# A loop hint on every engine: the closing branch of each loop is announced at the head of its body

## The reference

```
x = _layernorm(x + _L0_attn_ref(x, L0_attn_W), axis=-1)
x = _layernorm(x + _L0_ffn_ref(x, ...), axis=-1)
x = _layernorm(x + _L1_attn_ref(x, ...), axis=-1)
x = _layernorm(x + _L1_ffn_ref(x, ...), axis=-1)
```

```
h = dA_t * h + dBx_t
y = jnp.einsum('bdn,bn->bd', h, C_t)
```

## Time and profile before

| | |
|---|---|
| median of 3 runs | 2109.95 us |
| the three runs | 2109.95, 2128.29, 2106.08 us |
| the profiled execution, its own time | 2105.13 us |
| span, first to last instruction | 2103.4 us |
| mean granted TensorE clock | 0.852 |
| PE busy | 1455.2 us (69%) |
| DVE busy | 1404.4 us (67%) |
| POOL busy | 1285.9 us (61%) |
| ACT busy | 947.2 us (45%) |

### The profile page before, as it was taken

One profiled execution on the slowest core, in us unless ns is written; L12 is line 12 of the kernel. 1 busy time (PEld: TensorE's weight loads), 2 busy tenths in 40 slices (PEclk: granted clock), 3 DMA queues, 4 the chain that ended last, 5 costly groups with the idle time before them and its releaser, 6 DMA issues.

```text
span 2103.4 us, 22098 instructions
## 1 busy us (share of the span) xinstructions
PE 1455.2 (69%) x5345; PEld 863.5 (41%) x5345; DVE 1404.4 (67%) x2613; ACT 947.2 (45%) x1612; POOL 1285.9 (61%) x927
## 2 busy tenths in 40 slices
PE   4777400443898878888787898888766639968772
PEld 3655300331343333333333343333444418857661
DVE  3666597111799989989898898999844413335554
ACT  2443100112655665655565664565433317746461
POOL 2111201672998989988899998888645660053664
PEclk8999655556899999999999999999977759988996
DMA  5333481232322233222233222242023115857673
GB/s 151 110 107 109 129 217 27 39 41 55 123 89 101 108 117 116 80 88 75 107 116 116 85 82 77 105 147 106 5 83 109 48 46 160 228 159 212 191 222 85
DMA packets 215268, 229.96 MB, mean 109 GB/s; under 512 B 24456, under 2 KB 182216, under 8 KB 210760
## 3 DMA queue, kind: packets, MB, share of 16 engines
q1 hardware_dynamic: 192392, 203.28, 30.3%
q0 software_dynamic: 22784, 25.71, 6.0%
HBM read 168.37 MB, written 62.95 MB: 110 GB/s over the span
## 4 chain that ended last, share of the span: by engine, by line
PE 29%; issue 21%; DVE 19%; POOL 10%; another core or an unknown queue 8%; ACT 6%; DMA 3%; SPq 2%; DVEq 1%; POOLq 0%; ACTq 0%
DVE hst L1557 9%; PE bank L1208 8%; POOL dbx L752 5%; PE bank L1163 4%; DMA wv<-packed_weights 2%; PE bank L1073 2%; PE bank L1313 1%; PE bank L1299 1%; PE bank L1296 1%; POOL xe L686 1%; PE bank L1322 1%; PE bank L1161 1%; PE bank L1197 1%; DVE prod L1573 1%
## 5 line engine op out<-in xcount | busy, mean ns | idle before, releaser
L1557 DVE TENSOR_TENSOR_SCAN hst<-bank,dbx 128x512 f32<-128x512 f32 x512 | 592.3, 1206 | 55.6 <-ACT bank L949 40.9
L752 POOL TENSOR_TENSOR dbx<-u,ball 128x1024 f32<-128x1024 f32 x256 | 615.2, 2474 | 4.7 <-POOL u L783 2.8
L1208 PE MATMUL bank<-prod,ident 128*128 128x512 f32 x1024 | 502.9, 626 | 21.0 <-DVE prod L1573 17.8
L949 ACT ACTIVATE bank<-dt,aneg 128x511 f32<-128x511 f32 x512 | 347.5, 689 | 314.9 <-DVE hst L1557 314.7
L1208 PEld LDWEIGHTS bank<-prod,ident 128*128 128x128 f32 x1024 | 203.1, 201 | 252.0 <-issue 200.6
L1573 DVE TENSOR_TENSOR prod<-hst,bank 128x1024 f32<-128x1024 f32 x192 | 233.6, 1217 | 18.7 <-DVE hst L1557 13.4
L814 POOL DMA_INDIRECT yg<-expert_rows,row_of x128 | 125.0, 976 | 166.1 <-DMA expert_rows<-yu 116.1
L761 POOL TENSOR_TENSOR prod<-hst,call 128x1024 f32<-128x1024 f32 x64 | 158.9, 2482 | 70.4 <-DVE hst L1557 70.3
L1192 PE MATMUL bank<-parts,sel_c 128*128 128x512 bf16 x192 | 75.1, 392 | 113.5 <-DVE prod L1573 112.8
L1597 DVE SCALAR_TENSOR_TENSOR hg<-bank,wv,ha 128x256 f32<-128x256 f32 x96 | 42.1, 480 | 157.1 <-remote 56.7
L647 POOL TENSOR_SCALAR rstd<-mv 128x4 f32<-128x4 f32 x16 | 3.7, 228 | 199.9 <-DVE mv L1377 199.9
(11 more groups left out here) (262 smaller groups left out, 2915.8 us busy)
## 6 DMA issues: line engine op xcount, KB each, us to landing
ball<-b_rows SPq DMA_DIRECT2D x32, 2048.0 KB, 7.1
wv<-packed_weights SPq DMA_DIRECT2D x96, 322.0 KB
call<-b_rows SPq DMA_DIRECT2D x16, 1024.0 KB, 9.5
xr<-sorted_rows SPq DMA_DIRECT2D x48, 256.0 KB
expert_rows<-yu SPq DMA_DIRECT2D x48, 256.0 KB
xg_rows<-xg SPq DMA_DIRECT2D x16, 320.0 KB, 2.6
xt<-in_x SPq DMA_DIRECT2D x16, 256.0 KB, 3.0
xT<-in_xT SPq DMA_DIRECT2D x16, 256.0 KB, 3.2
```

What stands on the lines that cost most here:

```text
L752: gp.tensor_tensor(dbx[n % NDB][:, :, :], u[s.par][:, :, :], ball[:, n:n + 1, :].to_broadcast([P, NH, SEQ]), ALU.mult).then_inc(dbx_rdy, 1)
L949: act.activation(da_ps[h][:, 1:SEQ], dt_[s.par][:, h, 1:SEQ], ACT.Exp, scale=aneg[:, h, n:n + 1]).then_inc(da_rdy, 1)
L1208: last = mm(y_ps[:, h, :], ident[:, :], from_[:, h, :], start=False, stop=(n == NS - 1), skip_group_check=True)
L1557: dve.tensor_tensor_scan(h_of[:, h, :], da_ps[h][:, :], dbx[n % NDB][:, h, :], 0.0, ALU.mult, ALU.add).then_inc(scan_rdy, 1)
```

## The change

Every loop is built with the same loop function, called with a flag that it had left off. With the flag, the first instruction of the body is a branch hint: it names the branch that closes the loop, and with it the place that it jumps to. Nothing else is moved. All fourteen loops get one hint instruction in the body, which is carried out in every turn.

```diff
@@ schedule (Mamba, called by all five engines)
-    with eng.Fori(0, NB // 2 - 2) as j:
+    with eng.bass.Fori(0, NB // 2 - 2, engines=(eng.engine,), hint_back_edge=True) as j:
         for i in (2, 3):
             iteration(Seq(j, i + 1), Seq(j, i), Seq(j, i - 1), Seq(j, i + 2))
@@ stage 1: the same edit for sp, gp, act, pe and dve
-            with dve.Fori(0, NB // 2 - 1) as j:
+            with dve.bass.Fori(0, NB // 2 - 1, engines=(dve.engine,), hint_back_edge=True) as j:
@@ expert groups: the same edit for gp, act, pe and dve
-            with gp.Fori(0, E0 // EG // 2 - 1) as j:
+            with gp.bass.Fori(0, E0 // EG // 2 - 1, engines=(gp.engine,), hint_back_edge=True) as j:
```

More of the change, by code:

```diff
@@ L461, in _ @@
             load_x(Seq(0, 1))
-            with sp.Fori(0, NB // 2 - 1) as j:
+            with sp.bass.Fori(0, NB // 2 - 1, engines=(sp.engine,), hint_back_edge=True) as j:
                 for i in (1, 2):
@@ L651, in _ @@
             rsqrt(rstd, mv, Seq(0, 0), mv_rdy, rstd_rdy)
-            with gp.Fori(0, NB // 2 - 1) as j:
+            with gp.bass.Fori(0, NB // 2 - 1, engines=(gp.engine,), hint_back_edge=True) as j:
                 for i in (1, 2):
@@ L871, in _ @@
             stage1(Seq(0, 0), None)
-            with act.Fori(0, NB // 2 - 1) as j:
+            with act.bass.Fori(0, NB // 2 - 1, engines=(act.engine,), hint_back_edge=True) as j:
                 for i in (1, 2):
@@ L890, in group @@
                 act.activation(aeT[:, :, :], blk4(bank[4])[0:I0], ACT.Copy).then_inc(aeT_rdy, 1)
-            with act.Fori(0, E0 // EG // 2) as j:
+            with act.bass.Fori(0, E0 // EG // 2, engines=(act.engine,), hint_back_edge=True) as j:
                 for i in (0, 1):
@@ L1106, in _ @@
             stage1(Seq(0, 0), None)
-            with pe.Fori(0, NB // 2 - 1) as j:
+            with pe.bass.Fori(0, NB // 2 - 1, engines=(pe.engine,), hint_back_edge=True) as j:
                 for i in (1, 2):
@@ L1140, in group @@
                 last.then_inc(dn_mm, 1)
-            with pe.Fori(0, E0 // EG // 2) as j:
+            with pe.bass.Fori(0, E0 // EG // 2, engines=(pe.engine,), hint_back_edge=True) as j:
                 for i in (0, 1):
@@ L1515, in _ @@
             group(Seq(0, 1))
-            with dve.Fori(1, E0 // EG // 2) as j:
+            with dve.bass.Fori(1, E0 // EG // 2, engines=(dve.engine,), hint_back_edge=True) as j:
                 for i in (0, 1):
```

## The result

| | before | changed |
|---|---|---|
| median of 20 runs | 2111.34 us | 2105.72 us |
| lowest and highest | 2099.99 to 2131.35 us | 2089.98 to 2129.16 us |
| ratio, changed to before | | 0.9932, 95% interval 0.9906 to 0.9957 |
| profiled execution, own time | 2105.13 us | 2094.39 us |
| its span | 2103.4 us | 2092.3 us |

The ratio leaves out as slow what lies more than 1.5% above the fastest run of its kernel, which by the listed times is five of the changed kernel's 20 runs and none of the 20 before, so it flatters the change. All 20 runs against all 20 lie 5.6 us apart in the median (ratio 0.9973) and 5.9 us in the mean (0.9972; drawing anew from the listed times gives 0.9941 to 1.0004). The two profiled executions lie 11.1 us apart in span. So the times alone hardly tell the two kernels apart, and what follows rests on the profiles.

A forecast was written before the change was run, and what follows sets the result against it. No engine held a third of the chain; a fifth was "issue", including DVE's five Mamba branch stalls. A 13.4 us gain less 0.8 for hints gave 12.6 us, 2092.5 on the profile's level; forecast median 2096 us, range 2088 to 2112.

The forecast's parts named there:

- The place and the cause: DVE's taken branch in the Mamba loop waits 3.02 us for its missing head block, five times; other loops do not.
- The 11.1 us: Mamba loop: DVE's five idle times of 2.2 us before scans go; the scan starts when the product ends.
- What the sequence then takes: Mamba loop: twelve sequences of 61.21 us, 734.5 against 747.9, gain 13.4 us: 11.1 stall, 2.3 clock dips less catching up.
- My lower end, 8.2 us: Worst Mamba loop gain: clock dips stay and the catching up of 2.9 us is lost, 11.1 - 2.9 = 8.2.
- The hints: Hint instructions cost 0.4 us in stage 1 and 0.4 in the expert groups, sum 0.8, ends 0 and 2.7; moved code nothing.
- The sum: Whole kernel: 13.4 - 0.8 = 12.6 us less, 2092.5 us on the profile's level, 2096 taken as the median.
- a hint that does not help: Rival on DVE's Mamba loop: no or half help, median 2106 to 2111 us, or 2102 to 2105 with half saved; chance 0.27.
- The rule on prefetch: Skill's sentence that only the next block can be fetched; by it the sum would be +0.8 instead of -12.6 us.
- The rival that hurts: Stage 1 and expert groups: hint drops a needed block, 0.16 us steps become 3.02, 26 us in all; chance 0.1.
- Falling out of a loop may miss too: Part of the harm rival: leaving a hinted loop may also wait for a fetch, 3 times 2.9 us.

The follow-up runs named there:

- the runs with one hint: Hint only in DVE's Mamba loop, the other thirteen loops without, against the kernel before: loop 735.8 us against 747.9, ratio 0.9974.
- the other thirteen: Changed kernel without the hint in DVE's Mamba loop, hints in all other loops: loop 749.0 us, ratio 0.9991 to the kernel before.
- slot 0: Kernel before, no hint, head of DVE's Mamba loop padded to the first place of a fetched block: loop 737.0 us, ratio 0.9983.
- slot 100: Kernel before, no hint, head of DVE's Mamba loop padded to place 100 of a fetched block: loop 750.7 us.
- the written-out version: Mamba stage written out in Python on all engines, no loop and no hint there, against the kernel before: 12 sequences 723.7 us, ratio 0.9887.
- the second comparison: Changed kernel run again on another chip against the kernel before: median 1961.98 against 1967.89 us, ratio 0.9975, loop 735.9 us.
- the long body: 160 semaphore increments per turn added to DVE's Mamba loop, head on slot 64: loop 751.4 us without a hint, 736.7 us with it.
- the first four experiments: Hint only in DVE's Mamba loop, hints everywhere else, head on slot 0, head on slot 100: loops 735.8, 749.0, 737.0, 750.7 us.

## Why the prediction was right

**The place and the cause.** One loop of fourteen, on DVE, five times: the runs with one hint and with the other thirteen bear it out. The chain and the wait rows carried this; that the stall came from the taken branch was read from the fall-through at 1401.48. That a missing block was behind it was an inference from body sizes. The runs with slot 0 and slot 100 show that size alone does not decide: the same 336 instructions stall or not by where they start.

**The 11.1 us.** Gone in full. The branch takes 0.26 us to the hint, where I had set 0.16, and the scan follows `prod` as at any other step. ACT's decay and POOL's `dbx` were there in time, as forecast.

**What the sequence then takes.** Here a term was off, though the sum was not. I forecast twelve times 61.21 us and no dip of the clock that costs time: 13.4 us. Measured are eight sequences of 60.9 and four of 62.6, 10.3 us. I had tied the dips that cost 1.7 us to the stall, as they stood only behind stalls. They don't come from it: in the changed kernel they stand at the head of the sequences 4, 7, 10 and 13 alike, the first and third behind the branch, the others not. Against 61.21 the four cost 1.4 us more each, 5.5 together, and the eight 0.3 less each, 2.5 together: that is the 3 us between forecast and measurement. My lower end, 8.2 us, had let the dips stay, so the miss lies inside the range. In the written-out version the clock still dips (mean 0.94 in two of the sequences 2 to 5), yet the sequences take 60.2 to 60.5 us. What keeps the dips off the path there was not tried.

**The hints.** As instructions they cost what was set or less: 0.07 us from a hint to the next instruction on DVE, 0.06 on POOL, less than the register operations that bounded them. What the sum lacks is the fetch behind a hinted loop: about 2.3 us once on POOL ahead of the expert groups. I had put the code behind the hints at nothing, since I saw no 3 us pieces in straight code; with hints there is one.

**The sum.** 12.6 us forecast; 11.1 us between the profiled executions, of which 10.3 are the loop. The times say less: 5.6 us between the medians of 20 runs against 20, and by the second comparison, on another chip, 5 us (0.25% of 1968, interval 0.08 to 0.42%). The two agree with each other (0.9973 and 0.9975); the 0.9932 of the first comparison, 14 us, stands apart, for the reason given with the result. The loop's 10.3 us would be 0.9951 of 2105 us and 0.9948 of 1968 us. POOL's 2.3 us are part of what is lacking, since the other profiles have them without the luck of an early stage ahead; the rest is open, as no profile of the kernel before was taken on that chip. The median of 2105.7 us lies 9.7 above my 2096, inside the range. But the range took in nearly everything: 2105.7 is as near to what I had for a hint that does not help (2106 to 2111). The number did not decide between the two; the profiles did.

**The rule on prefetch.** I had set the Trainium skill's sentence that prefetch is purely sequential (Runtime: NRT & Kernel Launch, "Instruction fetch mechanics") against the change at 0.27. The measurement decides against it where a hint is given: the long body's head was fetched ahead of its branch. Its window of two blocks of 256, taken as each fetched on entry, does not agree with slot 0 either.

**The rival that hurts.** No turn of a loop that was free got slower. But "Falling out of a loop may miss too" came true in part: POOL's 2.3 us behind its loop of stage 1, and 2.8 to 3.1 us on DVE behind the Mamba loop in three of the six profiles with a hint there. I had priced three misses at 2.9 us each; in the changed kernel one was found.

## What to carry to other kernels

Look on the chain for "issue" pieces of about 3 us right behind a sequencer item with a loop's line, and count them: a hint is worth that number, less what the engine still had in hand (0.8 us each here). On loops without such a piece it gains nothing and can cost a late fetch behind the loop (2.3 us here), so give it only to the loop that stalls. A body that can be held whole may be cured by its place alone. Before a hint is tuned, ask whether the loop has to be one: where an engine's waits compare with registers, some of them cost about 0.2 us each on a path that an engine at 92% busy holds, and writing the stage out on that one engine gave as much again as the hint.

Before a small difference is read from a ratio, set the medians of all the runs beside it. Here 0.3% stood beside 0.7%.

## What the runs showed of the hardware

- A taken branch on DVE whose target had been pushed out cost 2.8 to 3.4 us to the next instruction, on ACT 2.4 to 2.6; with its target at hand 0.2 to 0.4 us, and 0.5 to 0.6 us in the long body with the hint.
- 336 instructions of a turn stayed in DVE's instruction memory from slot 0 of a block and did not from slot 100; a move of the head alone was worth as much as the hint (737.0 against 750.7 us).
- Straight code can wait for its instructions too: 2.8 to 3.1 us on DVE behind a hinted loop, and 3.2 to 3.4 us instead of 1.0 from one POOL instruction to the next, each time with an instruction packet within the gap.
- The same part of the program, from the first scan of sequence 14 to the end, took 701 to 702 us in the two profiles of the main comparison, 727 to 733 in those of the first four experiments, and 567 to 575 in the other eight. The rate of the DMA engines in the last stage differs with it between the first two and the last eight: 159 to 228 GB/s in the six slices of the page ahead of the last one in the kernel before (168 to 237 in the changed one), against 245 to 284 in five of them in the changed kernel's run on a fast chip. It does not tell the first two from the four at 727 to 733, which have 158 to 230 GB/s. The same instructions thus differ by 30 to 130 us, many times what was studied here. Whether the rate is the cause, and whether it also scatters the runs of one chip by 1%, was not tested.
